# A gated cross-attention kernel: score products split by batch, half of them late, and row-wise token tiles

## The reference

```python
q = (layernorm(x) @ Wq).reshape(b, n, 16, 64)
k = (context @ Wk * 64 ** -0.5).reshape(b, m, 16, 64)
v = (context @ Wv).reshape(b, m, 16, 64)
attn = softmax(einsum('bihd,bjhd->bhij', q, k))
x = x + tanh(g_xattn) * (einsum('bhij,bjhd->bihd', attn, v).reshape(b, n, 1024) @ Wo + bo)
h = layernorm(x)
top2 of softmax(h.mean(axis=1) @ gate_w), one choice of two experts per batch, weights w_e
x = x + tanh(g_ffn) * sum_e w_e * (gelu(h @ w1[e] + b1[e]) @ w2[e] + b2[e])
```

## Time and profile before

| | |
|---|---|
| median of three runs | 348.49 us (346.84 to 350.12) |
| the profiled execution | 348.49 us, its span 346.7 us |
| busy share of the span | PE 94%, PEld 79%, DVE 68%, ACT 48%, POOL 23% |
| mean granted TensorE clock | 0.987 |
| moved by DMA | 17.26 MB in 19678 packets |

### The profile page before, as it was taken

One profiled execution on the slowest core, in us unless ns is written; L12 is line 12 of the kernel. 1 busy time (PEld: TensorE's weight loads), 2 busy tenths in 40 slices (PEclk: granted clock), 3 DMA queues, 4 the chain that ended last, 5 costly groups with the idle time before them and its releaser, 6 DMA issues.

```text
span 346.7 us, 5736 instructions
## 1 busy us (share of the span) xinstructions
PE 325.5 (94%) x1810; PEld 274.0 (79%) x1810; DVE 234.7 (68%) x551; ACT 166.3 (48%) x580; POOL 78.8 (23%) x153
## 2 busy tenths in 40 slices
PE   7978999999999997688998999999999999999994
PEld 7965888889988996676786888888888888888883
DVE  0597879898799988777848737555575564643642
ACT  1627675667775744745436525444454442321320
POOL 1016335575365534337700000000000000000000
PEclk9999999999999998989999999999999999999998
DMA  7990000000000006007001560000000000110001
GB/s 259 399 91 4 0 2 0 3 1 2 1 1 2 2 9 234 2 0 243 2 0 43 202 212 31 0 0 0 2 1 0 0 0 0 61 62 0 32 30 61
DMA packets 19678, 17.26 MB, mean 50 GB/s; under 512 B 10949, under 2 KB 16198, under 8 KB 19526
## 3 DMA queue, kind: packets, MB, share of 16 engines
q1 hardware_dynamic: 19376, 16.43, 15.4%
q10 hardware_dynamic: 278, 0.53, 0.5%
HBM read 14.86 MB, written 2.10 MB: 49 GB/s over the span
## 4 chain that ended last, share of the span: by engine, by line
PE 72%; DVE 14%; ACT 7%; POOL 3%; issue 2%; DMA 2%; DVEq 0%; SPq 0%; ACTq 0%; POOLq 0%
PE ps L945 21%; PE ps L946 21%; PE ps L947 21%; ACT sx L495 5%; DVE mx L757 2%; PE ps L1046 2%; DVE pT_lo L721 2%; DMA wk_sb<-in_L_xattn_Wk_dram 2%; PE ps L966 2%; DVE a_lo L670 1%; DVE sm L730 1%; DVE w_lo L854 1%; PE ps L1012 1%; PE ps L1177 1%; ACT pT_hi L507 1%
## 5 line engine op out<-in xcount | busy, mean ns | idle before, releaser
L570 ACT ACTIVATE gel<-ps,b1sel 128x512 f32<-128x512 f32 x64 | 44.1, 688 | 108.5 <-PE ps L947 108.3
L905 DVE CAST h_hi<-gel 128x512 fp32r<-128x512 f32 x64 | 27.8, 434 | 71.6 <-ACT gel L570 71.3
L495 ACT ACTIVATE sx<-ps,mx 128x64 f32<-128x64 f32 x128 | 38.2, 327 | 34.5 <-DVE mx L757 34.5
L945 PE MATMUL ps<-h_hi,w_hi 128*128 128x512 f32 x128 | 51.0, 398 | 0.0
L945 PE MATMUL ps<-yT_hi,w_hi 128*128 128x512 f32 (+1 forms) x128 | 50.8, 397 | 0.0
L946 PE MATMUL ps<-yT_lo,w_hi 128*128 128x512 f32 (+1 forms) x128 | 50.4, 394 | 0.0
L947 PE MATMUL ps<-yT_hi,w_lo 128*128 128x512 f32 (+1 forms) x128 | 50.4, 394 | 0.0
L946 PE MATMUL ps<-h_lo,w_hi 128*128 128x512 f32 x128 | 50.3, 393 | 0.0
L947 PE MATMUL ps<-h_hi,w_lo 128*128 128x512 f32 x128 | 49.9, 390 | 0.0
L907 DVE TENSOR_TENSOR h_lo<-gel,h_hi 128x512 fp32r<-128x512 f32 x64 | 45.2, 706 | 2.2
L945 PE MATMUL ps<-vw,pT_hi 128*128 128x256 f32 x128 | 38.1, 298 | 5.6 <-DVE pT_lo L721 5.6
(11 more groups left out here) (135 smaller groups left out, 613.7 us busy)
## 6 DMA issues: line engine op xcount, KB each, us to landing
stage_w<-in_L_ffn_w_dram SPq DMA_DIRECT2D x8, 1024.0 KB, 6.2
out_dram<-xt SPq DMA_DIRECT2D x8, 256.0 KB, 2.5
xt<-in_x_dram SPq DMA_DIRECT2D x2, 512.0 KB, 9.0
wq_sb<-in_L_xattn_Wq_dram SPq DMA_DIRECT2D x1, 1024.0 KB, 8.9
wv_sb<-in_L_xattn_Wv_dram SPq DMA_DIRECT2D x1, 1024.0 KB, 10.6
wo_sb<-in_L_xattn_Wo_dram SPq DMA_DIRECT2D x1, 1024.0 KB, 13.5
xt<-in_x_dram SPq DMA_DIRECT2D x1, 1024.0 KB, 16.4
wk_sb<-in_L_xattn_Wk_dram ACTq DMA_DIRECT2D x1, 512.0 KB, 4.6
```

The source lines that it names most:

```text
L495: last = nc.scalar.activation(sx[:, par, c0:c0 + M], ps[:, 2 * par + 1, c0 - BANK:c0 - BANK + M], ACT.Exp, bias=mx[:, par, h:h + 1], accum ...
L570: nc.scalar.activation(gel[:, f % 2, :], ps[:, 4 + f % 2, :], ACT.Gelu, bias=b1sel[:, b, slot, f:f + 1]).then_inc(gelu_done, 1)
L905: nc.vector.tensor_copy(h_hi[:, f % 4, :], gel[:, f % 2, :]).then_inc(hhi_ready, 1)
L945: mm(acc, hi_w, hi_x, start=start, stop=False)
```

## The change

Six things change.

1. **Tokens.** `x` and `out` are taken row by row: tile t is tokens 128t to 128t+127, partition p token 128t+p. A row of a load or store is then one token, 1 KB.
2. **Loads.** The second half of Wk is issued by SP behind the first, not by ACT.
3. **Score products.** A group now belongs to one batch. `score_pair(i)` covers both column tiles of Wq for one batch, with 64 moving columns in 16 matmuls instead of 128 in 8. Setup makes the groups of batch 0 only (four instead of eight); those of batch 1 stand in steps 3 and 5, and the value groups of batch 1 move from steps 5 and 7 to 7 and 9. DVE's second x split stands between the second and third `a_lo`.
4. **Step 1 of ACT.** The exponentials of tile 1 stand in step 1 as those of all other tiles in theirs; before, they stood in step 2.
5. **Warm-up.** Three matmuls instead of one between `ctxT` and kT.
6. **Stores.** SP's eight stores are a loop instead of eight instructions.

```diff
-            half, ct, odd = i // 4, i // 2 % 2, i % 2
-            return w[:, ct, :].rearrange("p (b u m x) -> p u m b x", b=B, u=4, x=M)[:, 2 * half + odd, :, :, :]
+            b, half, odd = i // 4, i // 2 % 2, i % 2
+            c0 = b * HM + half * BANK + odd * (BANK // 2)
+            return w[:, :, c0:c0 + BANK // 2]
...
-                sp.dma_start(xt[:, b * TB + t0:b * TB + t1, :], x_rows[:, b, t0:t1, :]).then_inc(ld_x[i], 16)
+                sp.dma_start(xt[:, t0:t1, :],
+                             xf[t0 * P:t1 * P, :].rearrange("(t p) d -> p t d", p=P)).then_inc(ld_x[i], 16)
...
-            for i in range(NT // 2):
-                b, t = i * 2 // TB, i * 2 % TB
+            with sp.Fori(0, NT // 2) as i:
                 sp.wait_ge(x2_done, i + 1)
-                sp.dma_start(out_rows[:, b, t:t + 2, :], xt[:, i * 2:i * 2 + 2, :]).then_inc(stored, 16)
+                sp.dma_start(out[ds(i * 2 * P, 2 * P), :].rearrange("(t p) d -> p t d", p=P),
+                             xt[:, ds(i * 2, 2), :]).then_inc(stored, 16)
...
-                half, ct = i // 4, i // 2 % 2
+                b, half = i // 4, i // 2 % 2
                 banks = two_banks("A", i)
                 wait_group_read(pe, "kT", half)
                 wait_group_read(pe, "wqT", 2 * half + 1)
-                for m in range(4):
-                    for odd in range(2):
-                        r = slice(odd * DH, (odd + 1) * DH)
-                        last = mm(banks[odd][:, m * P:(m + 1) * P], wqT[r, 4 * half + m, ct * P:(ct + 1) * P],
-                                  kT_sb[r, 4 * half + m, :, :].rearrange("p b j -> p (b j)"), start=True, stop=True)
+                for ct in range(KD):
+                    for m in range(4):
+                        for odd in range(2):
+                            r = slice(odd * DH, (odd + 1) * DH)
+                            c0 = (ct * 4 + m) * M
+                            last = mm(banks[odd][:, c0:c0 + M], wqT[r, 4 * half + m, ct * P:(ct + 1) * P],
+                                      kT_sb[r, 4 * half + m, b, :], start=True, stop=True)
```

The table of late groups, before and now:

```diff
-        A0, V0 = [("A", i) for i in range(8)], [("vT", 0), ("vT", 1)] + [("VW", i) for i in range(4)]
-        LATE = {5: ("VW", 4), 7: ("VW", 6)}
+        A0, V0 = [("A", i) for i in range(4)], [("vT", 0), ("vT", 1)] + [("VW", i) for i in range(4)]
+        LATE = {3: ("A", 4), 5: ("A", 6), 7: ("VW", 4), 9: ("VW", 6)}
```

More of the change, by code:

```diff
@@ L38, in gated_cross_attention_moe_kernel @@
     assert 2 * DH == P and 2 * M == P and B * M == P and TOP == 2 and NCH == 2 and KD == 2
-    x_rows = x.rearrange("b (p t) d -> p b t d", t=TB)
-    out_rows = out.rearrange("(b p t) d -> p b t d", b=B, t=TB)
+    xf = x.rearrange("b s d -> (b s) d")
     cursor = [(nc.sbuf_base + 63) // 64 * 64]
@@ L248, in gated_cross_attention_moe_kernel @@
         number = {g: n for n, g in enumerate(groups)}
-        GRP_BANK = dict(zip(groups, [0, 1, 2, 3, 4, 5, 6, 0, 1, 2, 3, 4, 5, 6, 1, 4, 5, 6, 4, 5, 0] + [0, 1] * len(LATE)))
+        GRP_BANK = dict(zip(groups, [0, 1, 2, 3, 4, 5, 6, 0, 1, 2, 3, 4, 5, 6, 4, 5, 0] + [0, 1] * len(LATE)))
         assert all(s % 2 == 1 for s in LATE)
@@ L300, in _, with load_x @@
         def _(sp):
-            def load_x(i, b, t0, t1):
-                sp.dma_start(xt[:, b * TB + t0:b * TB + t1, :], x_rows[:, b, t0:t1, :]).then_inc(ld_x[i], 16)
+            def load_x(i, t0, t1):
+                sp.dma_start(xt[:, t0:t1, :],
+                             xf[t0 * P:t1 * P, :].rearrange("(t p) d -> p t d", p=P)).then_inc(ld_x[i], 16)
             sp.dma_start(ctx_sb[:, :], ctx_tokens.rearrange("b m d -> (b m) d")).then_inc(ld_ctx, 16)
-            sp.dma_start(wk_sb[:, :, 0:HD // 2], Wk.rearrange("(k p) n -> p k n", p=P)[:, :, 0:HD // 2]).then_inc(ld_wk[0], 16)
-            load_x(0, 0, 0, TB // 2)
+            for i in range(2):
+                cols = slice(i * HD // 2, (i + 1) * HD // 2)
+                sp.dma_start(wk_sb[:, :, cols], Wk.rearrange("(k p) n -> p k n", p=P)[:, :, cols]).then_inc(ld_wk[i], 16)
+            load_x(0, 0, TB // 2)
             sp.dma_start(wq_sb[:, :, :], Wq.rearrange("(k p) n -> p k n", p=P)).then_inc(ld_wq, 16)
             sp.dma_start(wv_sb[:, :, :], Wv.rearrange("(k p) n -> p k n", p=P)).then_inc(ld_wv, 16)
-            load_x(1, 0, TB // 2, TB)
+            load_x(1, TB // 2, TB)
             sp.dma_start(wo_sb[:, :, :], Wo.rearrange("(k p) n -> p k n", p=P)).then_inc(ld_wo, 16)
-            load_x(2, 1, 0, TB)
+            load_x(2, TB, NT)
             sp.dma_start(gate_sb[:, :, :], gate_w.rearrange("(k p) e -> p k e", p=P)).then_inc(ld_gate, 16)
@@ L422, in _ @@
         def _(act):
-            act.dma_start(wk_sb[:, :, HD // 2:HD], Wk.rearrange("(k p) n -> p k n", p=P)[:, :, HD // 2:HD]).then_inc(ld_wk[1], 16)
             act.dma_start(gg[:, 0:1], g_xattn.rearrange("(o n) -> o n", o=1)).then_inc(ld_g, 16)
@@ L476, in group @@
                     act.wait_ge(grp_done, n + 1)
-                    nc.scalar.activation(a_part(a_hi, i), bank.rearrange("p (m b x) -> p m b x", m=4, b=B),
+                    nc.scalar.activation(a_part(a_hi, i), bank.rearrange("p (k x) -> p k x", k=KD),
                                          ACT.Copy).then_inc(grp_hi, 1)
@@ L486, in _ @@
                 group(*g)
[L488 to L498, removed]
             def step(s, par):
@@ L509, in step @@
                                              ACT.Copy).then_inc(phi_ready, 1)
-                if s == 2:
-                    heads(1)
                 t = s - 1
@@ L540, in step @@
                         group(LATE[s][0], LATE[s][1] + odd)
-                if active(s) and s != 1:
-                    heads(s)
+                t = s
+                if active(t):
+                    act.wait_ge(max_done, t + 1)
+                    wait_pos(act, pT_done, 2 * (t - 1))
+                    for h in range(H // 2, H):
+                        c0 = h * M
+                        last = nc.scalar.activation(sx[:, par, c0:c0 + M], ps[:, 2 * par + 1, c0 - BANK:c0 - BANK + M],
+                                                    ACT.Exp, bias=mx[:, par, h:h + 1],
+                                                    accum_out=sm[:, par, h:h + 1])
+                    last.then_inc(head_done, 1)
                 if s == ROUTE0:
@@ L669, in group @@
                     dve.wait_ge(grp_hi, HI_AT[(kind, i)])
-                    nc.vector.tensor_tensor(a_part(a_lo, i), bank.rearrange("p (m b x) -> p m b x", m=4, b=B),
+                    nc.vector.tensor_tensor(a_part(a_lo, i), bank.rearrange("p (k x) -> p k x", k=KD),
                                             as_f32(a_part(a_hi, i)), ALU.subtract).then_inc(grp_dve, 1)
@@ L697, in _ @@
             x_split(0)
-            for g in A0:
+            for g in A0[:2]:
                 group(*g)
             x_split(1)
+            for g in A0[2:]:
+                group(*g)
             x_stats(1, range(TB // 2, TB))
@@ L991, in score_pair @@
                 wait_group_read(pe, "wqT", 2 * half + 1)
-                for m in range(4):
-                    for odd in range(2):
-                        r = slice(odd * DH, (odd + 1) * DH)
-                        last = mm(banks[odd][:, m * P:(m + 1) * P], wqT[r, 4 * half + m, ct * P:(ct + 1) * P],
-                                  kT_sb[r, 4 * half + m, :, :].rearrange("p b j -> p (b j)"), start=True, stop=True)
-                        if m == 3:
-                            last.then_inc(grp_done, 1)
+                for ct in range(KD):
[5 more added lines that the diff above has]
+                                      kT_sb[r, 4 * half + m, b, :], start=True, stop=True)
+                            if ct == KD - 1 and m == 3:
+                                last.then_inc(grp_done, 1)
             def value_pair(i):
@@ L1023, in _ @@
             group("ctxT", 0)
-            warm_up(1)
+            warm_up(3)
             group("kT", 0)
@@ L1032, in _ @@
             score_pair(0)
-            score_pair(2)
             def step(s, par):
@@ L1065, in step @@
                 if s == -1:
-                    score_pair(4)
-                    score_pair(6)
+                    score_pair(2)
                 t = s
@@ L1072, in step @@
                         wait_group_read(pe, "VW", 3)
+                    if t == TB:
+                        wait_group_read(pe, "A", 7)
                     if s - 1 in LATE:
@@ L1080, in step @@
                         if t < 2:
-                            wait_group_read(pe, "A", 4 * c + 3)
+                            wait_group_read(pe, "A", 3 if t == 1 else 2 * c + 1)
                         for k in range(KD):
@@ L1096, in step @@
                     pe.wait_ge(head_done, s)
-                    value_pair(LATE[s][1])
+                    (score_pair if LATE[s][0] == "A" else value_pair)(LATE[s][1])
                 if s in Y_AFTER:
```

## The result

The changed kernel takes 351.4 us (median of 17 runs, 349.49 to 353.89), the kernel before 347.5 us (17 runs, 346.76 to 350.12). The ratio is 1.0096, 95% interval 1.0078 to 1.0114: about 3.3 us slower, 2.7 to 4.0. The forecast was 351.0 us, within 347.6 to 353.2, most probably within 1%. The profiled execution of the changed kernel took 351.06 us with a span of 349.0; the spans of the two profiled executions differ by 2.3 us.

A forecast was written before the change was run, and what follows sets the result against it. Other engines, chiefly DVE, were taken to set the pace until about 44 us, then PE. Terms -2.2, -0.3, +1.0, +3.8 and +0.2 sum to +2.5 us on 348.5: 351.0 us, range 347.6 to 353.2.

The forecast's parts named there:

- signs of being wrong: Late pair's 32 records taking 1.0 us, PE waiting for `pT_lo` in steps 4, 6 or 10, or kT fast from its start.
- 1, four `a_lo` fewer: Setup: DVE makes four `a_lo` fewer, 2.4 us saved, less a 0.2 us wait; -2.2 us.
- 2, loads and warm-up: Before kT: Wk's second half behind the first and a filled pause start kT sooner; -0.3 us, bounds -0.7 and +0.4.
- 3, exponentials of tile 1: ACT, steps 1 and 2: `pT_hi` of tile 0 queues behind tile 1's exponentials, delaying the sum; +1.0 us.
- 4, two late pairs: Steps 3 and 5, PE without idle time: two score pairs at 1.9 us each; +3.8 us, bounds +1.9 and +4.0.
- 5, the end: Last store: 1 KB rows and SP's loop add time; +0.2 us, bounds 0 and +1.0.
- Rival B: Late pairs and kT: narrow matmuls cheap, PE at full pace before kT; -0.7 us, 347.8 us, chance 0.18.
- the choice between columns and instructions: Late pair on PE: 0.95 us if time goes by columns, 1.9 to 2.0 if by instructions; 1.9 taken.
- The wait for the transposes of x tile 1: Setup: DVE, free at 18.7, waits 0.2 us before the second x split for PE's transposes, ending near 18.9.
- The move of VW 6: From step 7 to 9: PE does the same 1.02 us before and after; 0, bounds 0 and +0.4 us.
- Rival C: Steps 3, 5 and 9: late copies break the ACT and DVE relay, up to 1.3 us each; 354.9 us, chance 0.18.
- Rival D: Loads and last store: 1 KB pieces tell, start at +0.4 and end at +1.0 us; 352.5 us, chance 0.06.

The follow-up runs named there:

- second look: The kernel before, unchanged, executed and profiled another time after a first such repeat; 345.97 us.
- two cut pairs: Two kernels against the changed kernel: late score pairs with 32 of 64 moving columns, or 64 of 128 weight columns; 350.88 and 348.12 us, one execution each.
- rows kernel: The kernel before with only x and out taken row by row in 1 KB pieces and the stores in a loop; 348.4 us, ratio 1.0002.
- start alone: The kernel before with only the second half of Wk from SP behind the first and three warm-up matmuls instead of one; 347.97 us, ratio 0.9984.
- split alone: The kernel before with only score products split by batch, half made late in steps 3 and 5, VW groups in 7 and 9; 349.46 us, ratio 1.0043.

## Why the prediction was right, and where its sum was not

The range held, the direction too, and the ratio of 1.0096 is within the 1% that was given the best chance. That 351.0 came within 0.4 us of 351.4 is partly luck: the 348.49 us it starts from is 1.0 above the median of 17 executions, and the sum is 0.8 below the 3.3 us measured. Of the signs of being wrong that the prediction names one came, kT at the fast pace from its start. Against the second look at the kernel before, whose kT ran at the same pace as that of the changed kernel, they measure:

| term | forecast | measured | from |
|---|---|---|---|
| 1, four `a_lo` fewer | -2.2 | -2.1 | tile 0's maximum behind wqT's start: 11.27 against 13.40 us |
| 2, loads and warm-up | -0.3 | +0.1 | wqT at 11.29 against 11.16 |
| 3, exponentials of tile 1 | +1.0 | +1.0 | maximum to sum, 5.46 against 4.44 |
| 4, two late pairs | +3.8 | +4.2 | handover to step 12: 68.68 against 64.43 |
| 5, the end | +0.2 | 0 | 3.8 us from DVE's last semaphore in both |
| sum | +2.5 | +3.2 | |

**Term 2 is the step that was mis-sized.** Wk's first half did arrive sooner (near 5.8 against 6.62) and kT began sooner, but with kT at the full pace its end is not what wqT waits for. Wq is, and it lands at 11.24 in the changed kernel against 11.12 in the second look. In the two kernels that have only the new loads, or these and the warm-ups, it lands at 11.33 and 11.41. I had read one execution as the kernel, and the 5.35 us of its kT as the rule; they were one of two cases. Rival B's mechanism (full pace before kT) showed in the trace after. It is at most a gain in part of the executions, since four of seven seen with one warm-up have it too. It also explains why the two profiled spans differ by less than the medians.

**Term 4**: the pair's 1.9 us was right (1.93), and the choice between columns and instructions came out as the rows of the transposes suggested. The two cut pairs show what sets it: the weight columns, not the moving ones. What was left out is the 0.2 us that the next matmuls need behind a late pair, 0.32 us instead of 0.12 for the first. With it the term is 4.2, above its upper bound of 4.0. The trace of before had it already: behind the group VW 4 the first matmul of the output takes 0.32 us as well, at 61.98.

**Terms 1 and 3** hold within 0.1 us. The wait for the transposes of x tile 1 was there as placed: DVE sits idle 0.22 us ahead of the second split, and `a_lo` 2 and 3 start at 18.81. **The move of VW 6** to step 9 cost nothing that shows: the 4.25 us more between handover and step 12 are the two pairs at 2.13. Rival C (ACT and DVE break behind the late copies) did not occur; PE is busy 44.00 of 44 us. Rival D falls with the rows kernel: the 1.5 us that it adds lie above the 1.1 us which that interval allows.

Do the parts timed apart add up? The ratios 1.0043 for the split, 1.0029 for the exponentials, 0.9984 and 1.0002 for start and rows give 1.0058, against 1.0096 measured. The intervals of the four parts, each 0.25 to 0.35% wide to either side, cover the difference, but that is a weak test. The lowest time of each kernel leaves out most of what differs between executions and is sharper:

| kernel | executions | lowest, us | above the kernel before |
|---|---|---|---|
| before | 35 | 345.88 | |
| start alone | 11 | 346.29 | +0.41 |
| exponentials alone | 12 | 346.93 | +1.05 |
| split alone | 12 | 348.13 | +2.25 |
| rows alone | 12 | 345.77 | -0.11 |
| sum of the four | | | +3.60 |
| changed | 17 | 349.49 | +3.61 |

The first five were timed on one chip. The changed kernel was timed beside 17 other executions of the kernel before, the lowest of which is 346.76, so that its own pair gives only 2.7. By the lowest times the start costs 0.4 us where the pair of traces has 0.1. Three warm-ups alone reach 345.91 and the new loads alone 346.33, against 345.97 for the kernel before beside them, which points at the loads: Wq lands later with them.

What stays open is why in some executions kT is slow with one warm-up: the pause ahead of it is 0.89, 0.98 and 2.35 us in the three slow cases and 0.39, 1.04, 1.35 and 1.57 in the four others, so its length alone is not it. Open too is what a slow kT brings with it: the value products ran at half pace in three of the four executions with a slow kT (the moved exponentials, the rows, no warm-ups) and in none of the ten with a fast one.

No kernel tried beats the kernel before by more than the measurement tells.

## What to carry to other kernels

Splitting a matmul into twice as many with half the moving columns saves nothing where the weight load sets the pace; count the loaded weight columns, not the streamed ones. Work moved out of a prologue pays only if it lands in idle time: here 2.1 us won ahead of the handover to PE were paid with 4.2 us behind it. Before costing a term of a microsecond from one profiled execution, look at a second one: a pace that changes within the first matmuls may be the execution's, not the kernel's.

## What the runs showed of the hardware

The column of the granted clock read 1.00 through the first 12 us of before, while the records of kT came at half the later pace (0.21 against 0.12 us, the two levels of 1.2 and 2.4 GHz) until about 10 us. In the rows kernel, whose kT began 0.7 us later, the same slow records have a column of 0.50 between 8 and 10 us. So in the first microseconds a 1.00 in the column can't be relied on, the distance between records can. A pause of 1.64 us ahead of the transposes of Wq went with a run at half pace behind it (3.63 us instead of 1.97, granted clock 0.50 from 12 to 14 us), one of 1.09 to 1.28 us did not; each is a single execution. The first full-height matmul behind a group of half-height ones took 0.32 us instead of 0.12. Stores in rows of 1 KB landed in 2.1 us where those of 2 KB took 2.5.
